# One product for all batches' last value rows, the output bias on GpSimd, and another order of calls up to the third group

## The reference

```python
x = x + jnp.tanh(g_xattn[0]) * _L0_xattn_ref(_layernorm(x, axis=-1), ctx_1024, 32, ...)
x = x + jnp.tanh(g_ffn[0]) * _L0_ffn_ref(_layernorm(x, axis=-1), ...)

# attention, per batch
q, k, v = query @ Wq.T + bq, mem_state @ Wk.T + bk, mem_state @ Wv.T + bv
scores = jnp.einsum('btd,bsd->bts', q, k) * scale      # all but the best 32 of 154 become -inf
ctx = jnp.einsum('bts,bsd->btd', softmax(scores), v)
return ctx @ Wo.T + bo

# feed-forward
h = jax.nn.relu(jnp.einsum('bsh,hi->bsi', hidden_states, W1) + b1)
return jnp.einsum('bsi,ih->bsh', h, W2) + b2
```

## Time and profile before

| | us |
|---|---|
| median of 3 runs | 253.32 (253.0 to 254.91) |
| profiled execution | 253.36 |
| its span, first to last instruction | 251.3 |
| TensorE busy in it | 246.8 |
| GpSimd busy | 170.4 |
| VectorE busy | 187.0 |
| ScalarE busy | 135.9 |

### The profile page before, as it was taken

The page is one execution under the profiler, slowest core; times in us unless marked ns, Lnnn a source line. Parts: engine busy times, 40 slices in busy tenths (PEclk is TensorE's granted clock), DMA queues, the critical chain, the costliest instruction groups (busy, mean ns, idle before and its releaser), DMA issues.

```text
span 251.3 us, 4726 instructions
## 1 busy us (share of the span) xinstructions
PE 246.8 (98%) x1470; PEld 216.9 (86%) x1470; DVE 187.0 (74%) x784; ACT 135.9 (54%) x292; POOL 170.4 (68%) x224
## 2 busy tenths in 40 slices
PE   8999999999999999999999999999999999999995
PEld 7867799999999988898889888898889888988884
DVE  3699999998998993689886988977556969332024
ACT  2579486576657476436660485526661485135720
POOL 3377988997977699674579567873869367745640
PEclk9999999999999999999999999999999999999999
DMA  7993011070301000109112400110011000100202
GB/s 206 379 416 148 0 25 27 1 278 17 125 4 42 0 4 0 42 5 323 52 42 86 126 1 3 42 43 3 0 43 42 3 1 4 39 3 0 83 0 83
DMA packets 6872, 17.21 MB, mean 68 GB/s; under 512 B 800, under 2 KB 2368, under 8 KB 6592
## 3 DMA queue, kind: packets, MB, share of 16 engines
q1 hardware_dynamic: 6848, 16.93, 19.1%
HBM read 12.44 MB, written 4.19 MB: 66 GB/s over the span
## 4 chain that ended last, share of the span: by engine, by line
PE 93%; DVE 5%; issue 1%; ACT 0%; DVEq 0%
PE y_ps L495 24%; PE z_ps L481 12%; PE z_ps L480 12%; PE z_ps L482 12%; PE y_ps L502 12%; PE sc_ps L406 6%; PE pt_ps L427 3%; PE att_ps L448 1%; PE att_ps L461 1%; PE att_ps L445 1%; PE att_ps L447 1%; PE att_ps L446 1%; PE y_ps L308 1%; PE pt_ps L461 1%; DVE picked L1234 1%; PE z_ps L315 1%
## 5 line engine op out<-in xcount | busy, mean ns | idle before, releaser
L1621 POOL TENSOR_TENSOR hid_lo<-hid,hid_hi 128x512 fp32r<-128x512 f32 (+1 forms) x80 | 85.3, 1078 | 50.9 <-ACT hid L960 50.5
L495 PE MATMUL y_ps<-w_both,hid_hi 128*128 128x512 f32 x256 | 83.4, 400 | 0.0
L959 ACT ACTIVATE hid_hi<-z_ps,small_in 128x512 fp32r<-128x512 f32 (+1 forms) x80 | 48.2, 603 | 49.0 <-PE z_ps L482 48.3
L480 PE MATMUL z_ps<-x2nt_hi,w_hi 128*128 128x512 f32 (+1 forms) x160 | 56.7, 354 | 0.0
L481 PE MATMUL z_ps<-x2nt_lo,w_hi 128*128 128x512 f32 (+1 forms) x160 | 55.6, 347 | 0.0
L482 PE MATMUL z_ps<-x2nt_hi,w_lo 128*128 128x512 f32 (+1 forms) x160 | 55.4, 346 | 0.0
L502 PEld LDWEIGHTS y_ps<-w_both,hid_lo 128*128 128x128 f32 x248 | 46.6, 188 | 9.2
L502 PE MATMUL y_ps<-w_both,hid_lo 128*128 128x256 f32 x248 | 52.2, 279 | 0.0
L1292 DVE SCALAR_TENSOR_TENSOR x<-y_ps,tanh_g,x 128x256 f32<-128x256 f32 x64 | 26.8, 477 | 33.4 <-PE y_ps L502 32.4
L960 ACT ACTIVATE hid<-z_ps,small_in 128x512 f32<-128x512 f32 (+1 forms) x80 | 47.9, 599 | 0.0
L495 PEld LDWEIGHTS y_ps<-w_both,hid_hi 128*128 128x128 f32 x256 | 42.7, 188 | 4.0 <-DVE x L1292 0.3
(11 more groups left out here) (147 smaller groups left out, 359.1 us busy)
## 6 DMA issues: line engine op xcount, KB each, us to landing
x_ring<-x SPq DMA_DIRECT2D x8, 512.0 KB, 6.0
out<-x SPq DMA_DIRECT2D x15, 256.0 KB, 2.0
xt_in<-x_t SPq DMA_DIRECT2D x7, 512.0 KB, 4.8
w_in<-w SPq DMA_DIRECT2D x2, 1024.0 KB, 10.5
wkq_in<-w_kq SPq DMA_DIRECT2D x1, 514.0 KB, 3.4
wvo_in<-w_vo SPq DMA_DIRECT2D x1, 513.0 KB, 6.6
xt_in<-x_t SPq DMA_DIRECT2D x2, 256.0 KB, 5.7
ctx_in<-ctx_t SPq DMA_DIRECT2D x1, 462.0 KB, 9.6
```

What stands on the lines that cost most here:

```text
L480: mm(dst, w1_hi[:, k, cols], hi[:, k, toks], start=k == 0, stop=False)
L495: last = mm(y_ps[t % 3][:], hid_hi[:, q % RING, tile_of_unit(g, j)], w2_both[:, c, :], start=c == 0, stop=c == KF - 1)
L959: func(hid_hi[:, q % RING, cols], z_ps[q % 2][:, cols], ACT.Relu, bias=b1[:, c:c + 1]).then_inc(hid_hi_made, 1)
L1621: nc.gpsimd.tensor_tensor(hid_lo[:, q % RING, cols], hid[:, q % FULL_RING, cols], hid_hi[:, q % RING, cols], ALU.subtract).then_inc(hid_lo ...
```

## The change

The rests of all four batches now stand in one tile `rest_ctx`, batch b in columns 32 b and on, and `values_of(1)` makes the values of all four at once, with the bias row in each. For the first batch, whose rows must stand threefold, ScalarE writes the 32 rows a second time and VectorE (`first_rest_to_lo`) makes the low part; the other three are moved as before, from the new rows and as soon as these are copied. `values_of(5)` is gone, and with it one of ScalarE's copies. `bo` is added to the first row of `wo_bv` by a second GpSimd addition, so that the product with ones that added it is gone. And the calls stand in another order: from the first score bias and the loads behind the seventh on to `layer_one(1, 1, 4)` on TensorE, and about as far on the other engines. From there on the order is unchanged.

```diff
         def _(sp):
             def move_rests():
-                sp.wait_ge(vals_copied, B + 2)
+                sp.wait_ge(vals_copied, 2)
                 for b in range(1, B):
                     for r in range(3):
-                        sp.dma_start(stacked[32 * r:32 * (r + 1), b - 1, :], values[32 * (b - 1):32 * b, B + 1, :]).then_inc(rest_moved, 16)
+                        sp.dma_start(stacked[32 * r:32 * (r + 1), b - 1, :], values[32 * b:32 * (b + 1), 1, :]).then_inc(rest_moved, 16)
...
-            load_xt(1)
-            load_w1()
             load_ctx(1)
             load_x(1)
+            load_w1()
+            load_xt(1)
             load_w2()
...
             def fold_value_bias():
-                pe.wait_ge(wo_bv_added, 1)
+                pe.wait_ge(wo_bv_added, 2)
                 pe.wait_ge(key_bias_made, 1)
-                mm(y_ps[0][:, 0:D], ones[:], wo_bv[:, 1, :], start=True, stop=False)
-                pe.wait_ge(small_loaded, 16)
-                mm(y_ps[0][:, 0:D], ones[0:1, :], bo[0:1, :], start=False, stop=True).then_inc(value_bias_ps_made, 1)
+                mm(y_ps[0][:, 0:D], ones[:], wo_bv[:, 1, :], start=True, stop=True).then_inc(value_bias_ps_made, 1)
...
-                    rows = first_rest[:, k, :] if n == 1 else other_rest[:, k, :] if n == B + 1 else ctx_in[:, k, first_row:first_row + P]
-                    last = mm(dst, rows, wvo[:, k, :], start=k == 0, stop=k == KD - 1 and not is_rest)
+                    rows = rest_ctx[:, k, :] if n == 1 else ctx_in[:, k, first_row:first_row + P]
+                    last = mm(dst, rows, wvo[:, k, :], start=k == 0, stop=k == KD - 1 and n != 1)
...
-                    pe.wait_ge(vals_lo_made, 2 if a < PER_BATCH else 4)
+                    if a < PER_BATCH:
+                        pe.wait_ge(first_rest_repeated, 1)
+                        pe.wait_ge(first_rest_lo_made, 1)
+                    pe.wait_ge(vals_lo_made, 1 if a < PER_BATCH else 3)
...
             def copy_values(n):
                 act.wait_ge(vals_ps_made, n + 1)
+                if n == 1:
+                    func(vals_rest[0:32, 0, :], vals_ps[n][0:32, 0:D], ACT.Copy).then_inc(vals_hi_made, 1)
+                    func(vals_rest[32:64, 0, :], vals_ps[n][0:32, 0:D], ACT.Copy).then_inc(first_rest_repeated, 1)
+                else:
+                    func(vals_hi[:, max(n - 1, 0), :], vals_ps[n][:, 0:D], ACT.Copy).then_inc(vals_hi_made, 1)
                 func(values[:, n, :], vals_ps[n][:, 0:D], ACT.Copy).then_inc(vals_copied, 1)
...
+            def first_rest_to_lo():
+                dve.wait_ge(vals_hi_made, 2)
+                dve.wait_ge(vals_copied, 2)
+                nc.vector.tensor_tensor(vals_rest[64:96, 0, :], values[0:32, 1, :], vals_rest[0:32, 0, :],
+                                        ALU.subtract).then_inc(first_rest_lo_made, 1)
...
-            def stack_first_rest():
+            def place_first_rest():
                 pool.wait_ge(ctx_loaded[0], 16)
-                for r in range(3):
-                    for k in range(KD):
-                        last = nc.gpsimd.tensor_copy(first_rest[:, k, 32 * r:32 * r + SR], ctx_in[:, k, P:S])
-                    last.then_inc(rest_made, 1)
+                nc.gpsimd.tensor_copy(rest_ctx[:, :, 0:SR], ctx_in[:, :, P:S]).then_inc(rest_made, 1)
...
             def add_wo():
                 pool.wait_ge(wo_bv_made, KD)
                 nc.gpsimd.tensor_tensor(wo_bv[:, 1, :], wo_bv[:, 0, :], wo_bv[:, 1, :], ALU.add).then_inc(wo_bv_added, 1)
+                pool.wait_ge(wo_bv_added, 1)
+                pool.wait_ge(small_loaded, 16)
+                nc.gpsimd.tensor_tensor(wo_bv[0:1, 1, :], wo_bv[0:1, 1, :], bo[0:1, :], ALU.add).then_inc(wo_bv_added, 1)
+                pool.wait_ge(wo_bv_added, 2)
...
             def first_values_to_lo():
                 pool.wait_ge(vals_copied, 1)
                 nc.gpsimd.tensor_tensor(vals_lo[:, 0, :], values[:, 0, :], vals_hi[:, 0, :], ALU.subtract).then_inc(vals_lo_made, 1)
-
-                pool.wait_ge(vals_lo_made, 1)
-                pool.wait_ge(vals_copied, 2)
-                nc.gpsimd.tensor_tensor(vals_rest[64:96, 0, :], values[64:96, 1, :], vals_rest[64:96, 0, :],
-                                        ALU.subtract).then_inc(vals_lo_made, 1)
-                pool.wait_ge(vals_lo_made, 2)
```

More of the change, by code:

```diff
@@ L84, in gated_block @@
         vo_bias = sb("vo_bias", [P, D])
-        values = sb("values", [P, B + 2, D])
+        values = sb("values", [P, B + 1, D])
         stacked = sb("stacked", [96, B - 1, D])
@@ L565, in _ @@
             values_of(3)
-            values_of(4)
             transpose_x2n(0, 0)
+            bias_scores(1)
             scores(1, 1)
-            values_of(5)
             layer_one(0, 0, 0)
             layer_one(0, 0, 1)
-            transpose_picked(0, 1)
-            scores(2, 0)
-            layer_two(0, 0, 0)
+            values_of(4)
             layer_one(0, 0, 2)
             layer_one(0, 0, 3)
+            transpose_picked(0, 1)
+            layer_two(0, 0, 0)
+            layer_two(0, 0, 1)
+            layer_two(0, 0, 2)
             attend(0, 1)
@@ L579, in _ @@
             layer_one(0, 0, 5)
-            layer_two(0, 0, 1)
-            layer_two(0, 0, 2)
-            layer_two(0, 0, 3)
+            scores(2, 0)
             layer_one(0, 0, 6)
             layer_one(0, 0, 7)
+            layer_two(0, 0, 3)
             transpose_x2n(0, 1)
             layer_two(0, 0, 4)
+            layer_two(0, 0, 5)
             transpose_picked(1, 0)
-            layer_two(0, 0, 5)
             layer_two(0, 0, 6)
+            layer_two(0, 0, 7)
             layer_one(0, 1, 0)
@@ L593, in _ @@
             layer_one(0, 1, 2)
-            layer_two(0, 0, 7)
             layer_one(0, 1, 3)
+            layer_two(0, 1, 0)
             layer_one(0, 1, 4)
+            layer_one(0, 1, 5)
             scores(2, 1)
-            layer_two(0, 1, 0)
-            layer_one(0, 1, 5)
+            layer_one(0, 1, 6)
+            transpose_x2n(1, 0)
+            layer_one(0, 1, 7)
             layer_two(0, 1, 1)
-            transpose_x2n(1, 0)
             layer_two(0, 1, 2)
             layer_two(0, 1, 3)
-            layer_one(0, 1, 6)
-            layer_one(0, 1, 7)
+            layer_two(0, 1, 4)
             transpose_picked(1, 1)
-            layer_two(0, 1, 4)
-            layer_two(0, 1, 5)
+            scores(3, 0)
             layer_one(1, 0, 0)
             layer_one(1, 0, 1)
+            layer_two(0, 1, 5)
             attend(1, 1)
@@ L614, in _ @@
             layer_two(0, 1, 7)
-            transpose_picked(2, 0)
             layer_one(1, 0, 3)
             layer_one(1, 0, 4)
-            scores(3, 0)
             layer_two(1, 0, 0)
@@ L621, in _ @@
             transpose_x2n(1, 1)
+            transpose_picked(2, 0)
             layer_one(1, 0, 5)
@@ L979, in _ @@
             w1_to_hi(0)
+            w1_to_hi(1)
+            copy_keys(1, 0)
+            copy_keys(1, 1)
             w2_to_hi(0)
-            copy_keys(1, 0)
-            exps(0, 1)
-            copy_keys(1, 1)
-            copy_score_bias(1)
-            w1_to_hi(1)
             w2_to_hi(1)
             copy_values(2)
+            x2nt_to_hi(0, 0)
             copy_values(3)
-            copy_values(4)
-            x2nt_to_hi(0, 0)
-            copy_rest(0, 1)
+            exps(0, 1)
+            copy_score_bias(1)
             relu(0, 0, 0)
             relu(0, 0, 1)
+            copy_rest(0, 1)
+            relu(0, 0, 2)
             pt_to_hi(0, 1)
-            copy_values(5)
-            exps(1, 0)
-            relu(0, 0, 2)
             relu(0, 0, 3)
@@ L1000, in _ @@
             relu(0, 0, 5)
+            exps(1, 0)
             relu(0, 0, 6)
+            relu(0, 0, 7)
+            x2nt_to_hi(0, 1)
             copy_rest(1, 0)
-            x2nt_to_hi(0, 1)
-            relu(0, 0, 7)
             pt_to_hi(1, 0)
+            copy_values(4)
             relu(0, 1, 0)
@@ L1341, in _ @@
             stats_x(1)
-            add_ctx(1)
+            first_rest_to_lo()
             pt_to_lo(0, 0)
             scale_scores(0, 1)
+            first_residual()
+            add_ctx(1)
+            normalise_second()
+            scale_scores(1, 0)
             topk_round(0, 1, 0)
-            first_residual()
+            x2nt_to_lo(0, 0)
             topk_round(0, 1, 1)
-            scale_scores(1, 0)
-            normalise_second()
             topk_round(0, 1, 2)
             topk_round(0, 1, 3)
-            x2nt_to_lo(0, 0)
             pick(0, 1)
@@ L1364, in _ @@
             x2nt_to_lo(0, 1)
-            topk_round(1, 1, 1)
+            stats_x(2)
             pt_to_lo(1, 0)
-            topk_round(1, 1, 2)
+            output(0, 0)
             scale_scores(2, 0)
             residual(1, 0)
-            output(0, 0)
+            topk_round(1, 1, 1)
+            topk_round(1, 1, 2)
             topk_round(1, 1, 3)
+            scale_scores(2, 1)
+            x2nt_to_lo(1, 0)
```

(2 more changed lines are left out.)

76 lines of the change are left out of this document (33 added, 43 removed).

## The result

The changed kernel is a little slower, not faster: 254.78 us median (253.95 to 255.75, 15 runs) against 253.82 (252.75 to 254.91, 15 runs) of the kernel before beside it. The ratio is 1.0037 [1.0021, 1.0052], or 0.9 us. The forecast was 252.7 and the range ended at 254.0. The profiled execution took 254.37 us with a span of 252.6.

What follows compares the result with a forecast made beforehand. TensorE, busy 246.8 of 251.3 us, was taken as the bound, with all effects before some 45 us. The sum -2.01 + 0.55 + 0.65 + 0.25 + 0.2 - 0.3 = -0.66 us gave 252.7, range 251.0 to 254.0.

Steps and rivals of the forecast that it cites:

- the last one of the sum: After 45 us every product is the same; moved calls up to the third group cost nothing while other engines keep ahead.
- second rival: GpSimd holds the second half's pick, pick(0, 1), to 2.47 us instead of 0.65; 254.2 us, chance 0.08.
- third rival: Gain lost between 45 and 100 us as TensorE waits for hid_lo; 253.3, or up to 254.0 us, chance 0.15.
- What is removed from TensorE: Dropped output bias product, 0.62 us, and second product for the remaining value rows, 1.39; together 2.01 us saved.
- The bias on GpSimd: TensorE's wo_bv product waits for a second, one-row GpSimd addition of 0.73 us: 0.55 us of new wait.
- The wait before the first transpose: Before transpose_x2n(0, 0) TensorE waits for the norm chain: +0.65 us, plus 0.25 for add_ctx(1) delaying the norm.
- The transpose of the second half: Transpose at 31.46, waiting for picked: 0.3 us of loss in place of 0.6, so -0.3 us.

Runs made afterwards that it cites:

- e8: Kernel before the change with only VectorE's pick(1, 1) moved behind scale_scores(2, 1) and x2nt_to_lo(1, 0); 255.2 us, 1.0063 to the kernel before.
- e1: Changed kernel with pick(1, 1) on VectorE back right behind its last top-k round; 253.17 us, 0.9967 to the kernel before.
- e2: Changed kernel with GpSimd's add_b2(0, 1) and add_b2(1, 0) moved behind hid_to_lo(0, 1, 7), pick(1, 1) left late; 254.56 us, 1.002 to the kernel before.
- e6: e5 with topk_round(0, 1, 0) ahead of normalise_second in VectorE's gap and x2nt_to_lo(0, 0) one round later; 252.23 us, 0.9946 to the kernel before.
- e7: e1 with the output bias added by TensorE's product again, GpSimd's one-row addition gone; 253.58 us, 0.9999 to the kernel before.
- e5: e1 with bias_scores(1) ahead of the first transpose, values_of(4) ahead of the first layer, copy_score_bias(1) behind copy_values(2); 252.87 us, 0.9975 to the kernel before.
- e3: Changed kernel with add_ctx(1) on VectorE moved from behind the first residual to before pt_to_lo(0, 0); 254.73 us, 1.0045 to the kernel before.

## Why the prediction was wrong

**The step that failed** is the last one of the sum: after 45 us "only the place of some calls up to the third group differs; I cost that at nothing as long as the other engines keep ahead". With it fails what it rests on: that all that the change can move lies before some 45 us, and that from the transpose at 31.46 on an edit on the other four engines can't matter by itself. In e8 only VectorE's order is changed, behind 50 us, and it costs 1.6 us. One of these places was `pick(1, 1)` beside `add_b2`. It cost 1.87 us in the trace, by the stretch that the changed kernel and e1 share, 1.8 by their ratios and 1.6 by e8. I had the mechanism in hand, with its price of 1.39 against 0.31, and in the second rival tied it to `pick(0, 1)` alone. The third rival named the stretch and even an exchanged pair of calls that makes a wait of its own, but allowed it no more than 254.0, 0.6 us above the kernel before, and thought otherwise of `hid_lo` and of giving back a gain. Both were given small chances, and neither was followed through the tables of VectorE and GpSimd for every pick that the change moves.

The Trainium skill's rule in "SBUF — State Buffer", section "Who interferes with whom", that a VectorE instruction with two inputs in SBUF and a GpSimd one that reads it exclude each other, agrees with all of this: 0.31 us alone, 1.4 beside `add_b2`, 1.96 beside the 1.93 us operation of e2.

**What is removed from TensorE**: right. The 1.39 us of the other rests are gone, and the bias product's place shrank from 1.15 us to 0.54: 2.0 us by start distances, as forecast.

**The bias on GpSimd**: right in kind, wrong in size. GpSimd and TensorE, changed kernel:

```profile
11.23 0.72 POOL L1532 TENSOR_TENSOR wo_bv<-wo_bv 128x256 f32<-128x256 f32 x1 [1.16 <-ACT wo_bv L868]
...
12.03 0.63 POOL L1535 TENSOR_TENSOR wo_bv<-wo_bv,small_in 1x256 f32<-1x256 f32 x1
```

One row of 256 takes 0.63 us, between the 0.73 that I took and the 0.53 that the prediction worked out as an estimate from the Trainium skill's "GPSIMD Engine Reference", section "2.1 Instruction dispatch". It ends at 12.66, and TensorE's product starts at 12.71 without a wait in its row. The first addition began 0.19 us earlier than before and TensorE's start-up was 0.26 later in this execution (its first scores at 9.81 against 9.55), which I couldn't count on. In e6, whose start-up was quick (first scores at 9.24) and whose first addition began later (11.65), the wait is 0.46, near the 0.55 forecast. So the term lies between 0 and 0.5 by the execution. Of the seven kernels with this addition only e6 shows the wait in its profile, and e7 too fits a term near 0.

**The wait before the first transpose**: right place and cause, forecast 0.9 more with `add_ctx`, measured 1.2 more (1.41 lost where about 0.2 was lost before). The hold by `add_ctx(1)` was 0.40, near its upper end. The chain of VectorE and GpSimd, changed kernel:

```profile
21.17 0.48 DVE L1249 SCALAR_TENSOR_TENSOR x<-att_ps,inv_denom,x_ring 128x256 f32<-128x256 f32 x1
...
23.11 0.70 DVE L1168 SCALAR_TENSOR_TENSOR ctx_u<-ctx_in,u_col,ctx_u 128x462 f32<-128x462 f32 x1
23.27 0.59 POOL L1593 TENSOR_SCALAR norm<-mv 128x2 f32<-128x2 f32 x1 [0.43 <-DVE mv L1261]
...
24.90 0.68 POOL L1602 TENSOR_SCALAR x2n<-x,norm 128x256 f32<-128x256 f32 x1
```

The transpose came at 25.64, as good as the 25.6 that I had with `add_ctx`, but that is partly luck. The first attention came at 20.39 instead of 20.80, since the bias cost nothing, and the residual behind it at 21.17 instead of 21.5. The chain from there was longer by as much: 0.40 for the hold where I took 0.25, and 0.79 from the norm to the end of GpSimd's `x2n` (24.79 to 25.58) where I counted VectorE's 0.55. TensorE was ready 0.4 us earlier for a transpose that came no earlier, so the wait took again about half of what the bias gave more. And e5 shows that this wait doesn't simply add to the time: with most of it covered the kernel was no faster, since `pick(0, 1)` came no earlier.

**The transpose of the second half**: the prediction's 0.6 us of loss before set the time to the next scores against how long four transposes last, and not against their distance of starts, 0.44 (18.20 to 18.64). By starts 0.9 us were lost before and 0.5 now, a gain of 0.4 where I had 0.3. The second rival didn't happen: the picks at 30.61 and 31.22 took 0.68 and 0.84, beside `hid_lo`.

Put together for the profiled executions: +1.01 measured (254.37 against 253.36). Less 1.87 for `pick(1, 1)` and 0.26 of start-up that any execution can have, it is -1.12, where the forecast was -0.66; e1 measures -0.84 by its ratio, with -1.27 to -0.41 by the interval. So for what it counted the sum had the right sign and came near, in part by errors that cancel: 0.55 too much for the bias, 0.3 too little for the wait, 0.1 too little gained at the transpose. The error that turned the result is the call that it did not count. The prediction was also wrong to take one per cent, 2.53 us, for what can be told from no change: with 15 runs on each side the interval of the ratio is 0.15% wide either way, and a change of 0.4% is clear of it.

## What to carry to other kernels

When an order table changes, follow every VectorE operation with two SBUF inputs through both engines' tables and ask which GpSimd operation it will meet; a pick of 0.31 us became 1.4 by moving past two calls, and moving GpSimd's operation instead only led to a meeting at the next pick. A dropped product is worth its time only if it covered no chain: here 0.6 of 2.0 us arrived with the old order. A wait that is covered ahead of the next late operation reappears there (e5), so shorten the chain as well, as with work put into a gap of the engine that is waited for (e6).

## What was not expected of the hardware

The first real products, eight of 257 columns on line 315, do not take the same time in all executions of the same start of program. e6 and e3, timelines of TensorE:

```profile
4.16 2.00 PE L315 MATMUL z_ps<-wkq_in 128*128 128x257 f32 x8
```

```profile
4.18 3.33 PE L315 MATMUL z_ps<-wkq_in 128*128 128x257 f32 x8
```

The group of eight lasts 2.00 us in the one and 3.33 in the other. Start to start, a product of them takes about 0.22 us or about 0.43, and it is the number of those at 0.43 that varies. The granted clock is given as 1.00 (the level of 2.4 GHz) from 4 to 8 us in both, behind the same warm-up products. The longer distance is twice the shorter, as if those products ran at the lower level of 1.2 GHz, but no row shows that level there, and why is open. It means that two single profiles can differ by up to 1.3 us at their start for nothing that the change does, and that only medians of several runs tell a difference of this size.
